# q kept as two tensors, rounded part below and remainder above on the partitions, in a fused gated-attention and feed-forward kernel

## The reference

```python
q, k, v = x @ Wq, x @ Wk, x @ Wv                 # (B, L, H, Dh), H = 16, Dh = 8
gk = log_sigmoid(x @ Wgk1 @ Wgk2 + bgk2) / 16
def step(state, inp):                            # scan over the 512 tokens
    qt, kt, vt, gt = inp
    state = state * exp(gt)[..., None] + vt[..., None] * kt[..., None, :]
    return state, einsum('bhvk,bhk->bhv', state, qt)
out = (out - mu) / sqrt(var + 1e-5) * gamma + beta
x = layernorm(x + (out * silu(x @ Wg)) @ Wout)
h = silu(x @ w1.T * s1) * (x @ w2.T * s2)
h = gelu(h @ h1.T * t1); h = gelu(h @ h2.T * t2)
x = layernorm(x + h @ w3.T * s3)
```

## Time and profile before

| | |
|---|---|
| median of 3 runs | 193.87 us (193.68 to 195.78) |
| the profiled execution | 193.71 us, of which the span from first to last instruction is 191.9 us |
| PE busy | 162.0 us, 84% of the span, 790 matmuls |
| PE weight loads | 124.0 us, 65% |
| DVE busy | 147.9 us, 77%, 301 instructions |
| ACT busy | 117.5 us, 61% |
| POOL busy | 113.8 us, 59% |
| L499, L500 (replicating q) | 32 matmuls each, 14.9 and 12.6 us busy |

### The profile page before, as it was taken

One profiled execution on the slowest core, in us unless ns is written; L12 is line 12 of the kernel. 1 busy time (PEld: TensorE's weight loads), 2 busy tenths in 40 slices (PEclk: granted clock), 3 DMA queues, 4 the chain that ended last, 5 costly groups with the idle time before them and its releaser, 6 DMA issues.

```text
span 191.9 us, 2751 instructions
## 1 busy us (share of the span) xinstructions
PE 162.0 (84%) x790; PEld 124.0 (65%) x790; DVE 147.9 (77%) x301; ACT 117.5 (61%) x188; POOL 113.8 (59%) x94
## 2 busy tenths in 40 slices
PE   1859988969499997999999699999987999799840
PEld 1638656849387774878768487677856866567630
DVE  1398886988788997998999997899999685512360
ACT  4633649898037725378682556768454688979623
POOL 8989589919706689580677688427782313470011
PEclk9999999999979999999999999999999999999996
DMA  3999700000000000000000010000000100002002
GB/s 119 332 419 405 274 3 0 0 0 3 0 3 0 0 2 0 3 2 0 0 0 0 0 41 14 0 0 0 3 0 0 56 0 0 0 0 60 0 3 58
DMA packets 6191, 8.65 MB, mean 45 GB/s; under 512 B 513, under 2 KB 5026, under 8 KB 5666
## 3 DMA queue, kind: packets, MB, share of 16 engines
q1 hardware_dynamic: 5602, 5.60, 9.1%
q0 software_dynamic: 576, 2.88, 3.9%
HBM read 7.43 MB, written 1.05 MB: 44 GB/s over the span
## 4 chain that ended last, share of the span: by engine, by line
PE 25%; DVE 18%; issue 8%; ACT 5%; POOL 4%; DVEq 1%; POOLq 0%; ACTq 0%
PE ffn L600 8%; PE ffn L591 8%; DVE state L994 5%; DVE y L1005 2%; DVE y L1009 2%; DVE f_lo L1091 1%; ACT f_hi L831 1%; PE ffn L569 1%; DVE o_acc L1012 1%; DVE ffn L1080 1%; PE att L526 1%; POOL u_tok L313 1%; PE ffn L574 1%; ACT f_hi L839 1%; POOL o_rstd L332 1%
## 5 line engine op out<-in xcount | busy, mean ns | idle before, releaser
L354 POOL TENSOR_TENSOR f_lo<-full,f_hi 128x512 fp32r<-128x512 f32 x20 | 26.0, 1315 | 30.4 <-DVE full L1080 19.5
L994 DVE TENSOR_TENSOR_SCAN state<-gate,att 128x512 f32<-128x512 f32 x32 | 38.4, 1210 | 3.0 <-PE att L515 3.0
L839 ACT ACTIVATE f_hi<-ffn,vec_cols 128x512 fp32r<-128x512 f32 x32 | 22.1, 690 | 27.4 <-PE ffn L600 27.2
L591 PE MATMUL ffn<-f_hi,h_hi 128*128 128x512 f32 x128 | 36.7, 405 | 1.7 <-ACT f_hi L831 1.3
L600 PE MATMUL ffn<-f_lo,h_hi 128*128 128x512 f32 x128 | 35.6, 399 | 0.0
L591 PEld LDWEIGHTS ffn<-f_hi,h_hi 128*128 128x128 f32 x128 | 23.5, 188 | 8.7 <-ACT f_hi L831 3.0
L1091 DVE TENSOR_TENSOR f_lo<-ffn,f_hi 128x512 fp32r<-128x512 f32 x28 | 18.9, 687 | 12.4 <-ACT ffn L842 11.4
L600 PEld LDWEIGHTS ffn<-f_lo,h_hi 128*128 128x128 f32 x128 | 23.9, 188 | 5.8 <-DVE f_lo L1091 0.4
L313 POOL TENSOR_TENSOR u_tok<-kv_tok 128x1024 f32<-128x1024 f32 (+1 forms) x12 | 27.3, 2282 | 0.5 <-issue 0.4
L328 POOL TENSOR_TENSOR o_acc<-o_acc,y 128x512 f32<-128x512 f32 x16 | 20.6, 1290 | 7.9 <-DVE y L1005 7.8
L1005 DVE TENSOR_TENSOR y<-att,state 128x512 f32<-128x512 f32 x32 | 21.1, 671 | 0.0
(11 more groups left out here) (162 smaller groups left out, 318.6 us busy)
## 6 DMA issues: line engine op xcount, KB each, us to landing
h_raw<-in_hT SPq DMA_DIRECT2D x2, 1024.0 KB, 11.3
h_hi<-in_hT POOLq DMA_DIRECT2D x2, 1024.0 KB, 11.7
x_tok<-in_x SPq DMA_DIRECT2D x4, 256.0 KB, 5.0
out<-out_tok SPq DMA_DIRECT2D x3, 256.0 KB, 2.3
w_raw<-in_w12T SPq DMA_DIRECT2D x1, 512.0 KB, 4.6
w_hi<-in_w12T POOLq DMA_DIRECT2D x1, 512.0 KB, 8.1
xT_raw<-in_xT SPq DMA_DIRECT2D x1, 256.0 KB, 2.6
proj_raw<-in_proj SPq DMA_DIRECT2D x2, 128.0 KB, 2.3
```

The source lines that it names most:

```text
L354: nc.gpsimd.tensor_tensor(lo[:, o], full_block(layer, o), hi[:, o].bitcast(F32), ALU.subtract).then_inc(pool_rested, 1)
L591: nc.tensor.matmul(bank[:], h_hi[:, layer - 1, c, tile(o)], src_hi[:, c], start=(c == 0), stop=False)
L839: nc.scalar.activation(hidden[layer][0][:, o], bank[:], ACT.Gelu, scale=scales[:, 1 + layer, o:o + 1]).then_inc(gelu_hi_ready, 1)
L994: nc.vector.tensor_tensor_scan(state[:, k % 3], gate[:, b], A[2 + k % 2][:], 0.0, ALU.mult, ALU.add).then_inc(scanned, 1)
```

## The change

The tensors `q_hi` and `q_lo` (each 128 partitions) go. In their place stands `q_both`, with two halves for each row. Half 0 holds the depth channels 0 to 3 of every head, half 1 the channels 4 to 7, which are 64 channels each. In a half, the lower 64 partitions hold the rounded value of the 64 channels and the upper 64 their remainder. For that the host lays out Wq as two matrices of 128 columns, each with its 64 columns twice; PE projects each half (three passes) into a bank of its own; ACT rounds all 128 partitions; DVE overwrites the upper 64 by the remainder. `rep` has four matrices in place of eight, each with two ones in a column, and `replicate_q` is one pass in place of two. The waits that depend on q's banks are renumbered, and the second half of q takes banks that z, g and attention use too.

```diff
-        q_hi = sb("q_hi", [P, B, L], F32R)
-        q_lo = sb("q_lo", [P, B, L], F32R)
+        q_both = sb("q_both", [P, 2, B, L], F32R)
-        Q_BANK = (A[0], F[0], F[0], F[0])
+        Q_JOBS = ((A[0], F[3]), (F[0], F[1]), (F[0], A[1]), (F[0], A[1]))
-            sp.dma_start(proj_raw[:, 2:4], proj[:, 2:4]).then_inc(qg_w_loaded, 16)
+            sp.dma_start(proj_raw[:, 2:5], proj[:, 2:5]).then_inc(qg_w_loaded, 16)
                                     # project_z
+                if b == 1:
+                    pe.wait_ge(q_lo_ready, 2)
-            def project_q(b):
+            def project_q(b, half):
                 pe.wait_ge(proj_lo_ready, 3)
                 if b == 1:
-                    pe.wait_ge(z_log_ready, 3)
+                    pe.wait_ge(z_log_ready, 3 + half)
+                elif b >= 2 and half == 0:
+                    pe.wait_ge(q_lo_ready, 2 * b - 1)
                 elif b >= 2:
-                    pe.wait_ge(q_lo_ready, b)
-                project(b, 2, Q_BANK[b], q_ready)
+                    pe.wait_ge(*((y_ready, DH) if b == 2 else (q_lo_ready, 2 * b)))
+                project(b, 2 + half, Q_JOBS[b][half], q_ready)
             def project_g(b):
-                pe.wait_ge(*((z_log_ready, 4), (kv_copied, 2 * B), (kv_copied, 2 * B - 1), (q_lo_ready, B))[b])
+                if b == 0:
+                    pe.wait_ge(q_lo_ready, 4)
...
-                nc.tensor.matmul(q_bank(b, k)[:], rep[:, k], q_hi[:, b], start=True, stop=False)
-                nc.tensor.matmul(q_bank(b, k)[:], rep[:, k], q_lo[:, b], start=False, stop=True).then_inc(q_rep_ready, 1)
+                half, n = k // (DH // 2), k % (DH // 2)
+                nc.tensor.matmul(q_bank(b, k)[:], rep[:, n], q_both[:, half, b], start=True,
+                                 stop=True).then_inc(q_rep_ready, 1)
                                     # PE, first stretch
-            project_q(0)
+            project_q(0, 0)
...
             replicate_q(0, 0)
+            project_q(0, 1)
             replicate_q(0, 1)
...
                 elif k == 5:
                     project_kv(1)
-                    project_q(1)
+                    project_q(1, 0)
                 elif k == 6:
+                    project_q(1, 1)
                     project_kv(2)
-            project_q(2)
+            project_q(2, 0)
             project_g(0)
             project_kv(3)
+            project_q(2, 1)
             transpose_o(0)
...
-            project_q(3)
+            project_q(3, 0)
+            project_q(3, 1)
                                     # ACT
-            def round_q(b):
-                act.wait_ge(q_ready, b + 1)
-                nc.scalar.copy(q_hi[:, b], Q_BANK[b][:]).then_inc(q_hi_ready, 1)
+            def round_q(b, half):
+                act.wait_ge(q_ready, 2 * b + half + 1)
+                nc.scalar.copy(q_both[:, half, b], Q_JOBS[b][half][:]).then_inc(q_hi_ready, 1)
...
             gates(0)
+            round_q(0, 1)
...
             fold_beta()
+            round_q(2, 1)
             sum_lo(2)
             sum_lo(3)
-            round_q(3)
+            round_q(3, 0)
+            round_q(3, 1)
                                     # DVE
-            def rest_of_q(b):
-                dve.wait_ge(q_hi_ready, b + 1)
-                nc.vector.tensor_tensor(q_lo[:, b], Q_BANK[b][:], q_hi[:, b].bitcast(F32),
+            def rest_of_q(b, half):
+                dve.wait_ge(q_hi_ready, 2 * b + half + 1)
+                low = q_both[P // 2:P, half, b]
+                nc.vector.tensor_tensor(low, Q_JOBS[b][half][P // 2:P], low.bitcast(F32),
                                         ALU.subtract).then_inc(q_lo_ready, 1)
...
             scan(0, 1)
             read_out(0, 0)
+            rest_of_q(0, 1)
             rest_of_x(2)
...
-            rest_of_q(1)
+            rest_of_q(1, 0)
             scan(0, 7)
+            rest_of_q(1, 1)
             read_out(0, 6)
             read_out(0, 7)
             last_sums(0)
-            rest_of_q(2)
+            rest_of_q(2, 0)
...
             apply_gate(0)
-            rest_of_q(3)
+            rest_of_q(2, 1)
+            rest_of_q(3, 0)
+            rest_of_q(3, 1)
```

More of the change, by code:

```diff
@@ L294, in _ @@
             nc.gpsimd.affine_select(out=rep_v, in_=rep_v, compare_op=ALU.not_equal, fill=1.0, base=0,
-                                    pattern=[[-1, DH], [-DH, HEADS], [0, DH]],
+                                    pattern=[[-1, DH // 2], [-(DH // 2), HEADS], [0, DH]],
+                                    channel_multiplier=1).then_inc(rep_half, 1)
+            pool.wait_ge(rep_half, 1)
+            nc.gpsimd.affine_select(out=rep_v, in_=rep_v, compare_op=ALU.not_equal, fill=1.0, base=-P // 2,
+                                    pattern=[[-1, DH // 2], [-(DH // 2), HEADS], [0, DH]],
                                     channel_multiplier=1).then_inc(consts_ready, 1)
@@ L498, in replicate_q @@
                     pe.wait_ge(y_ready, DH * b + k - 1)
-                nc.tensor.matmul(q_bank(b, k)[:], rep[:, k], q_hi[:, b], start=True, stop=False)
-                nc.tensor.matmul(q_bank(b, k)[:], rep[:, k], q_lo[:, b], start=False, stop=True).then_inc(q_rep_ready, 1)
+                if k == DH // 2 and isinstance(b, int) and b == 0:
+                    pe.wait_ge(q_lo_ready, 2)
+                half, n = k // (DH // 2), k % (DH // 2)
+                nc.tensor.matmul(q_bank(b, k)[:], rep[:, n], q_both[:, half, b], start=True,
+                                 stop=True).then_inc(q_rep_ready, 1)
             def transpose_u(b, k):
@@ L891, in _ @@
             act.wait_ge(gk12_ready, 1)
-            nc.scalar.copy(proj_hi[:, 4], A[3][:, P:2 * P]).then_inc(proj_hi_ready, 1)
+            nc.scalar.copy(proj_hi[:, 5], A[3][:, P:2 * P]).then_inc(proj_hi_ready, 1)
             act.wait_ge(gk_loaded, 48)
@@ L895, in _ @@
             act.wait_ge(qg_w_loaded, 16)
-            nc.scalar.copy(proj_hi[:, 2:4], proj_raw[:, 2:4]).then_inc(proj_hi_ready, 1)
+            nc.scalar.copy(proj_hi[:, 2:5], proj_raw[:, 2:5]).then_inc(proj_hi_ready, 1)
             act.wait_ge(consts_ready, 6)
@@ L912, in _ @@
             copy_kv(1)
-            round_q(1)
+            round_q(1, 0)
             gates(3)
+            round_q(1, 1)
             copy_kv(2)
-            round_q(2)
+            round_q(2, 0)
             sum_lo(1)
@@ L1182, in _ @@
             log_gate(0)
-            rest_of_q(0)
+            rest_of_q(0, 0)
             rest_of_x(1)
@@ L1267, in laid_out @@
     x = get["attn_x"]
-    proj = np.stack([get[f"attn_{n}"] for n in ("Wk", "Wv", "Wq", "Wg")], axis=1)
+    heads, depth = 16, HID // 16
+    channels = np.arange(HID).reshape(heads, 2, depth // 2).transpose(1, 0, 2).reshape(2, HID // 2)
+    q_cols = [get["attn_Wq"][:, np.tile(channels[half], 2)] for half in range(2)]
+    proj = np.stack([get["attn_Wk"], get["attn_Wv"], *q_cols, get["attn_Wg"]], axis=1)
     cols = [get[f"ffn_{n}"].reshape(OB, HID) for n in ("w1_s", "w2_s", "h1_s", "h2_s")]
```

25 lines of the change are left out of this document (14 added, 11 removed).

## The result

The changed kernel takes 202.06 us (median of 4 runs, 201.31 to 203.85) against 194.08 for the kernel before (also 4 runs), a ratio of 1.042 with a 95% interval of 1.037 to 1.048. Disturbed executions are left out of the ratios, so one can differ a little from that of the medians. In a second comparison, with 6 runs, it took 201.73 us, ratio 1.042 (1.038 to 1.045). The forecast was 199.8: slower, as said, but the loss is 8 us and not 6. The profiled execution took 202.08 us with a span of 200.2; the sum of the prediction had 199.7 for it.

What follows compares the result with a forecast made beforehand. It took DVE to bound the rows' attention, while DVE, PE and ACT wait in turn in the first stretch. 193.7 + 0.1 + 1.8 - 0.2 + 2.5 + 1.8 = 199.7 us, median 199.8; range 197.7 to 202.1.

Steps and rivals of the forecast that it cites:

- The rows: Attention of rows 1 to 3: the saved passes lie beside the DVE chain, value 0; 5.6 us if the cover were gone.
- Point 1: First stretch, rounding the weights: DVE's remainder of q's and g's weights grows from 256 to 384 columns, +0.1 us.
- the upper bound of 1.17: Added us for the weights' remainder if the 2.34 us before were the operation's own, slowed pace.
- Point 2: First stretch: z of row 1 waits for DVE's remainder of row 0's second half of q, +1.8 us.
- A clock of 0.50 in row 0: Sign that the prediction is wrong: TensorE's granted clock reading 0.50, 1.2 GHz in place of 2.4, in row 0.
- Points 3 and 4: Row 0: one pass less before k = 5, -0.2 us; q's second half of row 1 delays the scan of k = 7, +2.5.
- Points 5 and 6: End of row 0's attention, then ACT's list, which decides when `add_x` starts (51.9 instead of 45.91); together +1.8 us.
- The passes that pay in the rows: Rival, chance 0.08: PE bounds the rows, so 5.6 us come back and the time is 194.2 us.
- The held remainder: Rival, chance 0.12: DVE's half-height remainder doesn't overlap its neighbours; five borders of 0.19 us, +0.95, 200.7 us.
- The clock at `project_q(1, 1)`: Rival, chance 0.13: TensorE's clock falls after PE idles some 2.4 us before row 1's second half of q; +1.9, 201.7 us.

Runs made afterwards that it cites:

- e6: The changed kernel with each replication of rows 1 to 3 issued twice, 24 passes more; 200.81 us, ratio 1.035.
- e5: The kernel before with the pass for q's remainder left out in rows 1 to 3, 24 passes fewer; 194.06 us, ratio 1.003.
- e4: The changed kernel with q's remainder on the lower 64 partitions and the rounded value on the upper ones; 201.69 us, ratio 1.037.
- e13: The changed kernel with the replications of k = 0 to 3 issued twice in rows 1 to 3, 12 passes more; 201.76 us, ratio 1.037.
- e14: The changed kernel with one unread pass ahead of each centering product of rows 1 to 3; 201.35 us, ratio 1.036.
- e2: The changed kernel with row 0's second half of q in bank F2 in place of F3; 200.13 us, ratio 1.033.
- e11: The changed kernel with four unread passes ahead of each centering product of rows 1 to 3; 201.27 us, ratio 1.040.
- e15: The changed kernel as it is, measured again with more runs; 201.73 us, ratio 1.042.

## Why the prediction was right, and where it was short

*The rows (value 0).* This is the step that failed. That the passes bring nothing was right: from the centering of row 1 to that of row 3 it is 69.76 us before and 69.81 in the profiled execution, DVE's share unchanged. But the term was put at 0 because the passes lie "beside the DVE chain", and TensorE's clock was not asked about there. In the changed kernel it falls behind one of the centering products, which costs 1.82 us in the profiled execution and 0.55 in the second profile; with 24 passes given back it doesn't fall (e6), and with 24 left out of the kernel before it does (e5). In the profiled execution that is 1.8 of the 2.4 us that the sum is short.

*Point 1 (+0.1).* Right. DVE's 384 columns end 0.40 us behind POOL (13.21), the 256 had ended 0.28 behind it: the same pace, so the upper bound of 1.17 is out. POOL ended 0.12 earlier in this execution, and the end is at 13.61 in both. The page SBUF — State Buffer of the Trainium skill, section "SBUF: two separate sides", has a VectorE operation with two SBUF inputs and a GpSimd operation that reads SBUF exclude each other for a whole instruction; both traces agree with it.

*Point 2 (+1.8).* Mechanism right: z waits 1.21 us, released by the remainder of q, and goes on at 21.22 (forecast 21.15). The size was off by the clock, which fell right behind this wait in some executions: scan of k = 3 at 26.54, forecast 25.8. A clock of 0.50 in row 0 was one of the prediction's own signs of being wrong. Where it stayed up, that scan stood at 25.88 to 25.90.

*Points 3 and 4 (−0.2, +2.5).* Right to 0.02 us: scan of k = 7 at 39.58 and 39.61 in the two profiles of the changed structure whose clock stayed at 1.00 in row 0. In the profiled execution 40.24, by the delay of point 2.

*Points 5 and 6 (+1.8).* Nearly right: +2.1. `o_acc` at 43.67 and 43.71 (forecast 43.4), `add_x` at 52.24 and 52.27 (51.9). The missing 0.3 is what two held borders cost (0.12 each): for `o_acc` the two around the remainder of row 1's second half, for `add_x` the first of these and the one ahead of the sum. ACT's table load came at 44.65 and its last rounding of q ended at 50.56 in the second profile (forecast 44.4 and 50.5), so ACT's list decided, as said. The pair sum took 0.69 us, as said too. What the point didn't name is the loop of row 3's second half through A1; it became the limit once the rest was repaired.

*The rivals.* The passes that pay in the rows: refuted by two kernels. The held remainder: true, 0.12 us a border. The clock at `project_q(1, 1)`: true in some executions. With the stall unfilled it fell there in the profiles of e4, e6, e13 and e14, not in the two of the changed kernel, e2 or e11; 1.3 to 1.5 us where it fell (forecast 1.9). I had made the rivals exclusive, at 0.12 and 0.13; both were at work, and the clock at three places of which I had named one. Forecast 199.7 for the profiled execution; + 0.3 for the borders, + 1.8 behind row 3's centering and + 0.25 for the fall in row 0 (some 0.65) less what the later fall at the start of the rows gave back (some 0.4) = 202.05, measured 202.08.

## What to carry over

Ask of every bank that an edit gives to a second tenant what the tenant's wait for the first one's reader holds up: two such waits cost 4.0 us here, and moving one projection and changing one bank took them away. A pass saved beside the chain that sets the end is worth nothing, and it can cost time through the engine's clock, as it did here. When a kernel's executions differ by 2 us, read the clock by stretch before taking one profile for the kernel.

## What I had not expected of the hardware

- The clock of TensorE falls at different places in executions of one kernel. In row 0 of the changed kernel it read 0.58 and 0.57 from 22 to 26 us in one profile and 1.00 in another (202.08 and 200.47 us).
- Removing 24 hidden passes of 0.235 us, by the change or by leaving them out of the kernel before, made it fall behind the end of an attention; 3 passes of 0.235 us, one for each row, were enough to be without that in the one profile taken. Why so few passes decide, and what exactly the chip counts, stays open: 12 passes elsewhere in the rows did as well, with the idle time of 1.98 us kept.
- PE idled for 2.35 us ahead of `project_q(1, 1)` in eight of the profiles, and the clock fell after it in four of them (e4, e6, e13, e14). Ahead of the z of row 1 it fell behind waits of 1.2 us (the profiled execution) and 1.5 us (e6, e14), and stayed up behind longer ones, of 1.7 to 2.2 us (e15, e11, e13, e4). An idle stretch by its length alone doesn't tell.
- The column of the granted clock can't be read by itself. From 14 to 16 us it reads 1.00 in the kernel before, while the passes start 0.42 us apart where they later start 0.235 apart. Read the spacing of the passes beside it.
